# A four-layer graph transformer on one core: where layer 0's second-moment mix is computed, the exponent's place in layer 2's edge pass, and who writes the joins' one-hots

## What is computed

```
layer 0 graph:  h = elu(gat(x, W1)); h = elu(gat(h, W2))        # two GAT convolutions, 4 heads of 64
  gat: e = leaky_relu(a_s[src] + a_d[dst]); ex = exp(e - segment_max(e))[dst]
       out = segment_sum(ex * h[src], dst) / segment_sum(ex, dst) + b
layer 0 mix:    p = einsum('nd,ne->de', k, v) / N per head (8 heads of 32); out = (q p) WfcT + bfc
layer 2 graph:  the same segment softmax with one head and an edge term in the score ("ee")
layer 3 graph:  two HGT layers ("hgt"), again with a segment softmax over the edges
```

## Time and profile before

| | before |
|---|---|
| median of 3 runs (lowest, highest) | 7486.76 us (7485.75 to 7492.47) |
| the profiled execution | 7480.89 us, span 7479.1 us, mean granted TensorE clock 0.856 |
| busy over the span | PE 68 %, PEld 48 %, DVE 64 %, ACT 38 %, POOL 47 % |
| l0_in, then the mix phase | to 839.7, then to 864.7 us |
| first GAT: pass, join, tail | 864.7 to 1451, to 1524.5, to 1578 |
| second GAT: pass, join, tail | 1578 to 2162, to 2235, to 2285.6 |
| renew f_in | 2285.6 to 2337 |
| ee pass, join | 3761 to 4352.5, to 4420 |

### The profile page before, as it was taken

The page is one execution under the profiler, slowest core; times in us unless marked ns, Lnnn a source line. Parts: engine busy times, 40 slices in busy tenths (PEclk is TensorE's granted clock), DMA queues, the critical chain, the costliest instruction groups (busy, mean ns, idle before and its releaser), DMA issues. The chain is left out here.

```text
span 7479.1 us, 108245 instructions
## 1 busy us (share of the span) xinstructions
PE 5106.3 (68%) x21553; PEld 3606.0 (48%) x21554; DVE 4782.9 (64%) x12016; ACT 2809.2 (38%) x6885; POOL 3492.6 (47%) x3516
## 2 busy tenths in 40 slices
PE   4763677767774967759666656967776867776764
PEld 4762444444444834548543345834444444444453
DVE  6875477677776168551556554169997459996453
ACT  2551355345524220012223212227775147772321
POOL 1775277447730267731167701136664046661014
PEclk9999877777777988979867778989998999997777
DMA  3442244334422943338334405947765157772036
GB/s 88 163 144 62 78 129 127 81 89 128 127 58 88 318 113 101 104 72 323 117 96 108 104 16 175 301 144 213 211 210 157 36 161 212 211 212 57 20 110 202
DMA packets 523816, 1021.67 MB, mean 137 GB/s; under 512 B 143645, under 2 KB 284498, under 8 KB 514846
## 3 DMA queue, kind: packets, MB, share of 16 engines
q0 software_dynamic: 191360, 489.21, 24.3%
q1 hardware_dynamic: 301663, 497.07, 20.8%
q10 hardware_dynamic: 30528, 32.52, 1.2%
HBM read 927.97 MB, written 90.27 MB: 136 GB/s over the span
## 5 line engine op out<-in xcount | busy, mean ns | idle before, releaser
L733 POOL DMA_INDIRECT l_hgt_ep_g<-l_tkm,l_hgt_ep_ix x832 | 922.6, 1109 | 440.7 <-PE l_hgt_ep_out L831 235.4
L744 POOL DMA_INDIRECT l_gat_ep_g<-l_gat_th,keep_e_src x832 | 861.6, 1036 | 433.8 <-issue 229.7
L831 PE MATMUL l_gat_ep_out<-l_gat_ep_g,l_gat_ep_here 128*126 128x264 f32 x1664 | 711.7, 572 | 140.1 <-DVE l_gat_acc L988 136.0
L831 PEld LDWEIGHTS l_gat_ep_out<-l_gat_ep_g,l_gat_ep_here 128*126 128x126 f32 x1664 | 393.0, 267 | 367.5 <-DVE l_gat_acc L988 299.0
L2438 DVE TENSOR_TENSOR f_moe_experts_yb<-f_moe_experts_py,f_moe_experts_b2s 128x256 f32<-128x256 f32 x208 | 88.3, 424 | 709.9 <-PE f_moe_experts_py L2421 687.6
L2389 POOL DMA_INDIRECT f_moe_experts_xg<-f_moe_tx,f_moe_tok x208 | 196.7, 945 | 734.6 <-PE f_moe_experts_px L2402 618.0
L831 PE MATMUL l_hgt_ep_out<-l_hgt_ep_g,l_hgt_ep_here 128*126 128x288 f32 x1664 | 499.5, 424 | 53.2 <-DVE l_hgt_ep_g L974 52.0
L2453 ACT ACTIVATE f_moe_experts_ht<-f_moe_experts_phid,f_moe_experts_b1b 128x128 f32<-128x128 f32 x848 | 241.3, 372 | 726.8 <-PE f_moe_experts_phid L2412 720.1
L872 ACT COPY l_gat_ep_stage<-l_gat_ep_out 30x264 f32<-30x264 f32 x832 | 307.5, 371 | 537.6 <-PE l_gat_ep_out L831 529.1
L525 POOL DMA_INDIRECT recs<-place_stage,place_pos x392 | 425.2, 1085 | 138.5 <-issue 117.7
L2710 POOL DMA_INDIRECT l_edges_g<-l_table,keep_e_src x416 | 409.7, 985 | 147.5 <-issue 120.3
(11 more groups left out here) (635 smaller groups left out, 11735.3 us busy)
## 6 DMA issues: line engine op xcount, KB each, us to landing
l_hgt_ep_hot<-locrow SPq DMA_DIRECT2D x208, 256.0 KB, 5.0
f_moe_experts_w1b<-in_L_ffn_w SPq DMA_DIRECT2D x32, 1024.0 KB
f_moe_experts_w2b<-in_L_ffn_w SPq DMA_DIRECT2D x32, 1024.0 KB
f_moe_experts_w1b<-in_L_ffn_w SPq DMA_DIRECT2D x64, 512.0 KB
f_moe_experts_w2b<-in_L_ffn_w SPq DMA_DIRECT2D x64, 512.0 KB
f_moe_experts_w1b<-in_L_ffn_W SPq DMA_DIRECT2D x56, 512.0 KB, 4.9
f_moe_experts_w2b<-in_L_ffn_W SPq DMA_DIRECT2D x56, 512.0 KB, 5.1
l_gat_ep_hot<-locrow SPq DMA_DIRECT2D x104, 256.0 KB
```

The costliest lines, as they stand in the source:

```text
L733: gp.indirect_dma_start(g[:, b % NB, j, 0:W], None, table, bass.IndirectOffsetOnAxis(ap=ix[:, b, j:j + 1].bitcast(U32), axis=0)).then_inc( ...
L744: gp.indirect_dma_start(g[:, k % NB, j, 0:W], None, table, bass.IndirectOffsetOnAxis(ap=idx[:, k * CT + j:k * CT + j + 1].bitcast(U32), ax ...
L831: pe.matmul(out[:, t % 4, 0:WO], here[:, b % 2, t, :], g[:, b, t, F:F + WO], start=True, stop=True).then_inc(s_out, 1)
```

## The change

- The accumulation of X^T X and the column sums leaves renew. It becomes `row_sums`, a hook at the head of the first GAT's edge pass: PE does all 100 products of both kinds before its first lookup, into the PSUM tile `found`, and waits until DVE has copied them out; DVE does that after its memset.
- `squared_mix` is no phase any more. Its five steps stand in the loop of the first GAT's tail, PE's at i = 6, 9, 12, 15 and 18, DVE's at i = 11, 14, 17, 20 and 23; POOL's mask and SP's seven loads stand at the head of the tail's queues.
- The constant row c is added by a hook at the head of the second GAT's pass, one DVE instruction over 125 x 6400 after the memset, in place of 25 in f_in.
- In the ee pass ACT takes the exponent before the first half of its copies.
- In every join the one-hots of odd tiles are made on ACT (four Abs and one Relu), there are four buffers in place of two, and the semaphores are split.

```diff
 # edge_pass
-                piped(act, NCH, [(1, take(0)), (0, exponent), (1, take(1))], NB)
+                piped(act, NCH, [(0, exponent), (1, take(0)), (1, take(1))], NB)
 # edge_join
+        minus = ph.sb("minus", [104, NT, J])
-        hot = ph.sb("hot", [104, 2, J, P])
+        hot = ph.sb("hot", [104, 4, J, P])
+            pe.wait_ge(part_s, 1)
             for t in range(NT):
-                pe.wait_ge(hot_s, t + 1)
+                pe.wait_ge(odd_s if t % 2 else even_s, t // 2 + 1)
 # ScalarE's queue
+            def one_hot(t):
+                if t >= 4:
+                    act.wait_ge(out_s, t - 3)
+                for j in range(J):
+                    act.activation(hot[:, t % 4, j, :], core.iota[0:104, 0:P], ACT.Abs, bias=minus[:, t, j:j + 1])
+                act.drain()
+                act.activation(hot[:, t % 4, :, :], hot[:, t % 4, :, :], ACT.Relu, bias=core.ones[0:104, 0:1], scale=-1.0).then_inc(odd_s, 1)
+            act.wait_ge(minus_s, 1)
+            one_hot(1)
+            one_hot(3)
             act.wait_ge(scaled, 1)
             act.activation(fac[:, 1:], fwd[:, :], ACT.Exp).then_inc(fac_ready, 1)
+            for t in range(5, NT, 2):
+                one_hot(t)
 # VectorE's queue
+            v.tensor_scalar(minus[:, :, :], at[:, :, :], -1.0, None, ALU.mult).then_inc(minus_s, 1)
             one_hot(0)
+            one_hot(2)
             for t in range(NT):
-                if t + 1 < NT:
-                    one_hot(t + 1)
-                put(t)
+                if t % 2 == 0 and t + 4 < NT:
+                    put(t)
+                    one_hot(t + 4)
+                else:
+                    put(t)
 # gat_tail
+                    if mixing is not None and i >= 6 and i % 3 == 0 and i // 3 - 2 < 5:
+                        mixing["tensor"](pe, i // 3 - 2)
+                if mixing is not None and i >= 11 and i % 3 == 2 and i // 3 - 3 < 5:
+                    mixing["vector"](v, i // 3 - 3)
 # renew, per tile (the copy at its end goes too)
-                            for k in range(2):
-                                pe.matmul(p_square[:, k, 0:D], of[:, t, 128 * k:128 * k + 128], of[:, t, :],
-                                          start=t == 0, stop=t == NT - 1, skip_group_check=True)
-                                mm = pe.matmul(p_square[:, k, D:D + 1], of[:, t, 128 * k:128 * k + 128], core.ones[0:P, 0:1],
-                                               start=False, stop=t == NT - 1, skip_group_check=True)
-                            mm.then_inc(s_square, 1)
+def row_sums(core, ph, found, xn, square):
+    def on_tensor(pe):
+        for t in range(NT):
+            for k in range(2):
+                pe.matmul(found[:, k, 0:D], xn[:, t, 128 * k:128 * k + 128], xn[:, t, :], start=t == 0, stop=t == NT - 1, skip_group_check=True)
+                mm = pe.matmul(found[:, k, D:D + 1], xn[:, t, 128 * k:128 * k + 128], core.ones[0:P, 0:1], start=False, stop=t == NT - 1, skip_group_check=True)
+        mm.then_inc(s_square, 1)
+        pe.wait_ge(s_taken, 1)
+    def on_vector(v):
+        v.wait_ge(s_square, 1)
+        v.tensor_copy(square[:, :, :], found[:, :, 0:D + 1]).then_inc(s_taken, 1)
+def constant_row(x, cvec):
+    def on_vector(v):
+        v.tensor_tensor(x[:, :, :], x[:, :, :], cvec[:, :].unsqueeze(1).to_broadcast([P, NT, D]), ALU.add)
 # layer0
-            renew(core, "l0_in", x, xn, onward={"w": w[0], ...}, square=square)
-            squared_mix(core, "l0_mix", hold, square, wkv, bkv, wqo, bq, bo, 32, 1.0 / N, s_mixer)
+        renew(core, "l0_in", x, xn, onward={"w": w[0], ...})
+        gat(core, "l0_gat1", g, th, onward=(w[1], brow[1], after), early=lambda ph_, found: row_sums(core, ph_, found, xn, square),
+            mixer=lambda ph_: squared_mix(core, ph_, hold, square, 32, 1.0 / N))
+        gat(core, "l0_gat2", g, after, x=x, early=lambda ph_, found: constant_row(x, hold[1]))
+    return {"mix": (hold[0], None)}
```

More of the change, by code:

```diff
@@ L708, in edge_pass @@
             ex = ph.sb("ex", [128, 2, CT])
-        mixing = early(ph) if early is not None else None
+        mixing = early(ph, found if kind != "ee" else None) if early is not None else None
         s_ix, s_parts = ph.sem("ix"), ph.sem("parts")
@@ L737, in _ @@
             else:
-                if mixing is not None:
+                if mixing is not None and "pool" in mixing:
                     mixing["pool"](gp)
@@ L748, in _ @@
         def _(sp):
-            if mixing is not None:
+            if mixing is not None and "sync" in mixing:
                 mixing["sync"](sp)
@@ L832, in total @@
                 return body
-            if mixing is not None:
+            if mixing is not None and "tensor" in mixing:
                 mixing["tensor"](pe)
@@ L873, in take @@
                 return body
-            if mixing is not None:
+            if mixing is not None and "act" in mixing:
                 mixing["act"](act)
@@ L1047, in _ @@
                 for j in range(J):
-                    mm = pe.matmul(p_out[:, t % 2, 0:WC], hot[:, t % 2, j, :], part[:, j, :], start=(j == 0), stop=(j == J - 1))
+                    mm = pe.matmul(p_out[:, t % 2, 0:WC], hot[:, t % 4, j, :], part[:, j, :], start=(j == 0), stop=(j == J - 1))
                 mm.then_inc(out_s, 1)
@@ L1411, in _ @@
             def _(sp):
+                if mixing is not None:
+                    mixing["sync"](sp)
                 for t in range(NT):
@@ L1801, in linear_mix, with renew @@
     return {"mix": (a, cvec if (q_b is not None or out_b is not None) else None)}
-def renew(core, name, x, xn, mix=None, part=None, fetch=None, norm=True, onward=None, keep=None, out=None, square=None):
+def renew(core, name, x, xn, mix=None, part=None, fetch=None, norm=True, onward=None, keep=None, out=None):
     wide = onward is not None
@@ L2130, in _ @@
                 last_on_vector(v)
-                v.drain()
-            if square is not None:
-                v.wait_ge(s_square, NT)
-                v.tensor_copy(square[:, :, :], p_square[:, :, 0:D + 1])
                 v.drain()
@@ L2620, in layer0 @@
+        renew(core, "l0_in", x, xn, onward={"w": w[0], "M": D + 8, "bias": brow[0], "dst": g, "table": th, "loads": []})
         after = core.dram("l0_gat2_th", (N, D + 4))
-        gat(core, "l0_gat1", g, th, onward=(w[1], brow[1], after))
-        gat(core, "l0_gat2", g, after, x=x)
-    return {"mix": hold}
+        gat(core, "l0_gat1", g, th, onward=(w[1], brow[1], after), early=lambda ph_, found: row_sums(core, ph_, found, xn, square),
+            mixer=lambda ph_: squared_mix(core, ph_, hold, square, 32, 1.0 / N))
```

241 lines of the change are left out of this document (131 added, 110 removed).

## The result

The changed kernel takes 7442.3 us (median of 4, 7432.12 to 7446.05) against 7487.92 us of the kernel before; the ratio is 0.9933, with a 95 % interval of 0.9921 to 0.9946. It is faster by 46 us, clearly more than the 0.2 % that can be told from none, but by half of what was forecast (97.5), and above the range of 7364 to 7426.

The account below looks back on a forecast made before the run. A different limit in each stage: PE in l0_in, POOL's gathers in the first GAT pass, DVE's wait for ACT's exponent in ee. Terms -27.5 + 8.5 - 25 + 8 - 4 + 5.5 - 42 - 21 = -97.5 gave 7389.3 us, range 7364 to 7426.

Parts of the forecast that it names:

- The sums' duration at the new place: Head of the first GAT pass: PE's sums delay the first chunk and POOL stalls 7.5 to 8.5; +8.5, from +4 to +20.
- The first rival: First GAT pass doesn't catch up, the delay of PE's sums is paid whole: +25 for +8.5, 7406; chance 0.11.
- The held gather: Head of the second GAT pass: the constant row's addition holds a gather, 6.43 us and not 0.95; +5.5 (0 to +6).
- the fourth rival: Second GAT pass: the addition doesn't stop the gather, 0 for +5.5, 7384; chance 0.05.
- The exponent first: Ee pass: DVE's wait for ACT's exponent goes, POOL becomes the bound and the saving saturates; -42, from -30 to -46.
- The second rival: Ee pass: the wait only moves, to ACT's copies after the exponent; of 42 only 10 stay, 7421; chance 0.12.
- The joins: Five joins: with every other one-hot off DVE, PE is the bound, 1.84 and 1.76 a tile; -21 (-8 to -26).
- The third rival: Joins: PE waits for ACT's one-hots, or 2.08 is its own pace; 0 for -21, 7410; chance 0.06.
- l0_in: Row sums out of l0_in: 24 tiles x 1.06, the copy and cold tiles at the start; -27.5, between -22 and -31.
- The mix phase: Before the first GAT pass: POOL's first gather no longer waits 24.75 us for the mix; -25 (-24 to -26).
- the tail: First GAT's tail: the mix's DVE work paid nearly in full, PE's lumps hold back some 3.5; +8 (+3 to +12).
- The fifth rival: Ee pass: DVE's denser work slows every gather, slower than before; at g = 1.3 7526; chance 0.02 with its kin.

Follow-up runs that it names:

- two loops: Changed kernel with the 50 products of X^T X first, then the 50 with one column of ones, at the first GAT pass's head: 7417.37 us.
- two loops with ones as weights: Changed kernel with sums in two loops, the second as 25 products of 256 columns with ones as weights, and constant row added from PSUM: 7389.21 us.
- The drain: Changed kernel with a drain between the memset and the constant row's addition at the second GAT pass's head: 8013.6 us, in a later group 7419.76 us.
- the old joins' loops: Changed kernel with the joins of the kernel before (all one-hots on DVE, two buffers): 8031.41 us, in a later group 7441.08 us.
- two loops, row from PSUM: Changed kernel with X^T X first, then the one-column products, and the constant row copied to PSUM and added from there: 7387.49 us, 0.9876 of the kernel before.

## Why the prediction was wrong

The direction and the parts that bind were right; of eight terms five were within a few us, and three were mis-sized by 27, 12 and 11, which is the whole error of 46 with the small ones (-6.5, -1.6 and +3.4) against each other. On the medians the forecast is 53 off; the other 7 lie in no term (6 between the terms' sum and the medians, 1 in the kernel before).

**The sums' duration at the new place (+8.5, measured +35.9).** The step that failed is "25 x 1.31 = 33 us, with a cold start 35 to 36". It carried a duration over from l0_in, where other wide products stood between the squares and the clock was 1.00, to a place where the squares stand alone. There they ran at 0.52 to the end: 63.1 us from PE's first product to DVE's copy. The bound named for it, +20 for "wholly cold", was too low as well: 25 x 2.56 = 64 us puts the first chunk's products some 28 us later than 36 would, and 8.5 + 28 = 36.5 is what came. A weak sign of it stood in the text: the mix phase, where PE worked without the stream of a pass or of l0_in, had a clock of 0.62, though PE also waited for DVE between its steps there. The Trainium skill, page "TensorE: Matmul & The Clock Gate", section "Part 1: The HAM clock gate (the "warmup" mystery)", says that the clock follows how busy PE has been recently. The busy time of the profile isn't the measure of that here: 62.24 of 64 us were busy at 0.52. What the measure is, no run shows.

The rest of the working held. With sums of 63.1, 41.1 and 34.8 us (the changed kernel, two loops, two loops with ones as weights) POOL stalled for 41.1, 19.3 and 13.0 us, so the ring of four buffers covers 22 us each time. The pass's gathers lasted 35.9, 15.6 and 9.1 us more than in the kernel before, so the pass makes up 4 to 5. With sums as short as the forecast had them (35 to 36) the cost is close to the forecast's (9.1 for 8.5). The first rival (the pass doesn't catch up, the delay is paid whole) named the right place but another cause: at 34.8 us of sums it would have cost 25, and 9.1 was measured.

**The held gather (+5.5, measured +17.3).** The mechanism was forecast, and the fourth rival (no gather held) falls. The size was off since the row came from ee's head, where a drain and a wait stand before the additions; here the addition follows the memset directly, and the gather is held through both: 14.14 - 0.95 = 13.2, and the pass lost 4 more. In the five other profiles outside the second group that have the same 14.1 us in one gather, the pass's gathers lasted 568.3 to 572.7 us, so the further loss is between nothing and 4, and its cause is open. The drain (6.85) shows that it is the addition behind the memset, not the memset. The hold would then begin when the addition is handed on, before the memset has even started; that is consistent with these rows but no run shows it by itself. The Trainium skill, page "SBUF — State Buffer", section "Who interferes with whom", has two SBUF inputs of the DVE instruction as the condition for contending with a GpSimd instruction that reads SBUF; the run with one operand in PSUM agrees (0.95 in all 14 gathers). The section's inference that tensor_tensor leaves descriptor generation alone is contradicted by 14.14 and 6.85.

**The exponent first (-42, measured -30.9).** The bound moved to POOL and the saving saturated, as the text said. The step that failed is the drain of the pass: "the last data lands about 3 us after its issue". At the end the DMA engines are full (0.99 for 0.41) and move 75 GB/s for 107, so the last data comes late. The score came 10.0 us after the last gather's start instead of 3.8, and from the last use of the exponent (4298.27) to the first put it took 34.3 for 30.4. The row for it was there: in the first GAT pass, already bound by gathers, the last score came at 1430.15, 8.4 after the last gather's start at 1421.8, and the join's first put 51.2 after it. A pass that becomes bound by gathers ends as another such pass does, with 47.7 here. Part of the 11 is 1.6 in the gathers themselves. The second rival (the wait moves to ACT's copies) has no row: DVE waits for ACT's copies 17 us in all.

**The joins (-21, measured -17.6).** The loops are shorter by 5.0, 5.4 and 5.7 in three joins, and by 0.9 and 0.6 in hgt's two, which is within the scatter of those. The loops run at 1.88, 1.86 and 1.75 a tile, so the pace read from hgt's products was right for ee and 0.03 low for GAT, and the half microseconds at the start weren't there. The third rival falls, with the old joins' loops back at 50.1, 50.1 and 47.3.

**The rest.** l0_in gained 34.0 instead of 27.5. Its tiles take 1.23, so the loop gave 27.1 for 25.4; the cold tiles at the start gave 4.5 for 1.4; and some 2.4 come from the seven loads, which the text had put at 0 and which shortened a wait in the phase before (13.04 to 9.98). The mix phase (-25.0), the tail (+8.2) and f_in (-5.6 at 1.73 a tile, so PE was not full at the 1.8 to 1.88 of the text) are as forecast or inside their bounds. The fifth rival (denser work slows the gathers) has nothing for it: ee's gathers lasted 530.7 for 529.1. The range was too narrow because its bounds were drawn around durations read in other places, and the two that broke had been carried over without their surroundings. With the first two faults taken away (two loops, row from PSUM) the kernel takes 7387.5 us.

## What to carry to other kernels

A duration of PE belongs to the stream that it was read in: when a step moves, ask what will stand between its products, and look for the stretch of the profile in which PE worked alone. Put wide products together and narrow ones last, or replace one-column products by wide ones with the narrow operand as weights. Beside POOL's gathers keep long DVE instructions to one SBUF operand, or put a drain before them; and take the tail of a stage that changes its bound from a stage that has that bound already. When loads leave a queue, look also at what waited behind them. And price an edit by its stages: medians of the same kernel in two groups lay 10 us apart here.

## What the hardware showed that was not expected

The order of the same 200 products decided the clock: 0.52 interleaved, 1.00 and then 0.50 in two loops (23.45 and 17.76 us). Interleaved in the same way, but with other wide products between the tiles, they ran at 1.00 in l0_in. A two-operand addition of 6.76 us on DVE held a gather for 14.14 us when it was queued directly behind a memset, for 6.85 behind a drain, and not at all with one operand in PSUM. At the end of a pass the DMA engines were 0.98 to 0.99 busy with 75 to 77 GB/s, where in mid-pass they moved 107 at 0.41. And one group of runs was 8 % slower: the kernel with the drain took 8013.6 us there and 7419.76 in another group, with first takes of l0_in at 868.4 and 772.0 and gathers of the two GAT passes and of ee of 703.9, 648.6 and 643.3 us for 594.8, 565.3 and 531.7. What differed between the two groups, the record doesn't say.
